# TensorE's order in the loop: value halves among the passes of the inverse, projections ahead of the turning of o, turning of x behind queries times keys

## The reference

```python
x_n = layernorm(x)                             # both parts read this
q, k, v = short_conv_silu(x_n @ Wq/Wk/Wv)      # causal convolution of 4 taps, then silu
beta = sigmoid(x_n @ Wb);  q, k = l2norm(q), l2norm(k)
# delta rule, per head, chunk by chunk, S carried:
A = inverse of (I + strictly lower part of beta k k^T);  u = A (beta v) - A (beta k) S
o = q S + (q k^T, lower part) u;   S = S + k^T u
# multi-scale branch on v: causal convolutions of 3, 15, 31 taps, kernel_mix, channel_mix
# gates: softmax(gelu([x_n, mean |.| of the three branches] @ w1 + b1) @ w2 + b2)
o = gates . (ms, o, v);  o = rms_norm(o);  attention = o @ Wo
# feed-forward: xr, xk = mixes of x_n and the token before
out = sigmoid(xr @ W_r) * (relu(xk @ W_k)^2 @ W_v)
y = x + attention + feed-forward
```

## Time and profile before

| | |
|---|---|
| runs shown | 3519.88 us median, 3506.42 to 3535.21 |
| profiled execution | 3516.6 us, its span 3514.4 us |
| busy share of the span | PE 95%, PE's weight loads 70%, DVE 90%, ACT 78%, POOL 23% |
| chain that ended last | PE 35%, DVE 22%, ACT 21%, issue 10%, DMA 9% |
| mean granted clock of TensorE | 0.98 |

### The profile page before, as it was taken

How to read it: one execution, slowest core, us unless ns; L and a number is a source line. 1 busy time by engine, 2 the same in 40 slices (tenths; PEclk the granted TensorE clock), 3 DMA queues, 4 the chain that set the end, 5 groups by cost and what they waited for, 6 DMA issues and landing times.

```text
span 3514.4 us, 70437 instructions
## 1 busy us (share of the span) xinstructions
PE 3333.0 (95%) x22880; PEld 2459.5 (70%) x22880; DVE 3165.4 (90%) x7841; ACT 2758.5 (78%) x9146; POOL 823.5 (23%) x1501
## 2 busy tenths in 40 slices
PE   7999999999999999999999999999999999999988
PEld 5666777667776677766777767777766777667764
DVE  6998999999988998999989989998999889999994
ACT  5777888778787777877778877788777788777875
POOL 2322221122221222212222112222112222122211
PEclk9999999999999999999999999999999999999999
DMA  6022211122211222112222112221112221122211
GB/s 186 18 40 51 51 35 38 29 51 51 48 29 24 51 51 50 31 32 40 51 51 41 35 26 51 51 50 32 37 33 51 50 47 31 31 44 51 45 30 21
DMA packets 188310, 154.96 MB, mean 44 GB/s; under 512 B 111804, under 2 KB 146108, under 8 KB 187688
## 3 DMA queue, kind: packets, MB, share of 16 engines
q0 software_dynamic: 31744, 79.70, 13.1%
q1 hardware_dynamic: 156200, 70.76, 7.6%
HBM read 51.34 MB, written 52.95 MB: 30 GB/s over the span
## 4 chain that ended last, share of the span: by engine, by line
PE 35%; DVE 22%; ACT 21%; issue 10%; DMA 9%; POOL 3%; SPq 0%; ACTq 0%; DVEq 0%; POOLq 0%
DVE my L1924 16%; PE dense L811 7%; DMA my<-prod 5%; PE dense L734 5%; PE dense L744 5%; PE dense L721 4%; ACT my L1361 3%; PE small L757 2%; DMA rows_out<-Bm 2%; ACT dense L1394 2%; PE cell L703 2%; PE cell L704 2%; POOL Xu L464 1%; DMA Bu<-rows_out 1%; PE cell L696 1%
## 5 line engine op out<-in xcount | busy, mean ns | idle before, releaser
L1924 DVE SCALAR_TENSOR_TENSOR my<-vT,mw,my 128x256 f32<-128x256 f32 x5408 | 2257.1, 482 | 41.1 <-DMA my<-prod 22.3
L422 POOL TENSOR_SCALAR vare<-xsq 128x2 f32<-128x2 f32 x32 | 6.0, 187 | 2037.0 <-ACT xsh L1104 2037.0
L811 PE MATMUL dense<-xsh,w 128*128 128x256 f32 x2016 | 474.5, 381 | 3.8
L811 PEld LDWEIGHTS dense<-xsh,w 128*128 128x128 f32 x2016 | 362.6, 190 | 70.9 <-ACT xr L1426 10.9
L1334 ACT ACTIVATE ka<-dense 128x512 f32<-128x512 f32 x64 | 38.2, 596 | 313.6 <-PE dense L721 313.6
L721 PE MATMUL dense<-xk,wfk 128*128 128x256 f32 x1024 | 249.9, 400 | 11.6 <-DVE xb L1992 10.9
L721 PEld LDWEIGHTS dense<-xk,wfk 128*128 128x128 f32 x1024 | 199.3, 199 | 65.1 <-issue 37.1
L574 PE MATMUL front<-xsh,wq 128*128 128x256 f32 x1024 | 238.2, 386 | 0.6 <-ACT raw L1142 0.6
L734 PE MATMUL dense<-wr,xr 128*128 128x512 f32 x512 | 235.1, 602 | 0.0
L574 PE MATMUL front<-xsh,wv 128*128 128x256 f32 x1024 | 229.9, 382 | 2.7 <-ACT xsh L1119 2.7
L574 PE MATMUL front<-xsh,wk 128*128 128x256 f32 x1024 | 228.2, 379 | 3.8 <-ACT raw L1142 3.8
(11 more groups left out here) (188 smaller groups left out, 6846.2 us busy)
## 6 DMA issues: line engine op xcount, KB each, us to landing
my<-prod POOLq DMA_DIRECT2D x160, 384.0 KB, 4.2
xa<-in_x SPq DMA_DIRECT2D x32, 512.0 KB, 4.4
rows_out<-Bm SPq DMA_DIRECT2D x64, 256.0 KB, 4.2
out<-xb POOLq DMA_DIRECT2D x32, 512.0 KB, 14.8
Yq<-units_out SPq DMA_DIRECT2D x128, 32.0 KB, 2.3
w<-in_w SPq DMA_DIRECT2D x1, 2048.0 KB, 16.2
Bu<-rows_out SPq DMA_DIRECT2D x32, 64.0 KB, 3.1
units_out<-Xu SPq DMA_DIRECT2D x32, 64.0 KB, 2.5
```

The costliest lines, as they stand in the source:

```text
L811: e.matmul(by_batch(o), w1[:, k, hs(2 * pair + c)], xsh[s % 2][:, k, :, 1:1 + P], start=(k == 0), stop=False)
L1924: i = e.scalar_tensor_tensor(o, vT[s % 2][:, c, :, off:off + P], mw[:, col:col + 1], o, ALU.mult, ALU.add)
```

## The change

On TensorE, within the loop only: state(i-2, 0) goes ahead of the second half of value_out(i-2, 1); beta_and_q_norm goes ahead of logits(i-2, 0); turn_tokens(i-1, 2) goes behind kernel_mix(i-1, 0); turn_x(i, 0) goes behind both query_key; key_state(i-1, 1) goes behind the fourth pair of projections; the fifth pair goes ahead of turn_o(i-2, 0); attend(i-2, 0, 0) goes ahead of turn_o(i-2, 1), and the two batches' halves of attend alternate; value_out(i-1, 0, 0) goes ahead of join_Z and its other half between half_W and half_X. In DVE's program adjacent calls of taps with adjoining ranges are written as one call. The programs of ACT, GpSimd and SyncE are not changed.

```diff
@@ -912,8 +912,8 @@
                 gate_out(i - 2, 1, 0)
                 gate_out(i - 2, 1, 1)
                 value_out(i - 2, 1, 0)
+                state(i - 2, 0)
                 value_out(i - 2, 1, 1)
-                state(i - 2, 0)
                 kernel_mix(i - 2, 3)
                 state(i - 2, 1)
                 channel_mix(i - 2, 0, 0)
@@ -933,21 +933,20 @@
                 turn_tokens(i - 1, 1)
                 hidden(i - 2, 3, 0)
                 hidden(i - 2, 3, 1)
+                beta_and_q_norm(i - 1)
                 logits(i - 2, 0)
-                beta_and_q_norm(i - 1)
                 logits(i - 2, 1)
-                turn_tokens(i - 1, 2)
                 turn_logits(i - 2)
                 turn_beta(i - 1)
                 kernel_mix(i - 1, 0)
+                turn_tokens(i - 1, 2)
                 gram(i - 1, 0)
                 gram(i - 1, 1)
-                turn_x(i, 0)
                 query_key(i - 1, 0)
                 query_key(i - 1, 1)
+                turn_x(i, 0)
                 turn_x(i, 1)
                 kernel_mix(i - 1, 1)
-                key_state(i - 1, 1)
                 project(i, 0, 0)
                 project(i, 0, 1)
                 project(i, 1, 0)
@@ -956,13 +955,14 @@
                 project(i, 2, 1)
                 project(i, 3, 0)
                 project(i, 3, 1)
-                turn_o(i - 2, 0)
+                key_state(i - 1, 1)
                 project(i, 4, 0)
                 project(i, 4, 1)
+                turn_o(i - 2, 0)
+                attend(i - 2, 0, 0)
                 turn_o(i - 2, 1)
-                attend(i - 2, 0, 0)
+                attend(i - 2, 1, 0)
                 attend(i - 2, 0, 1)
-                attend(i - 2, 1, 0)
                 attend(i - 2, 1, 1)
                 ffn_key(i - 1, 0, 0)
                 ffn_key(i - 1, 0, 1)
@@ -972,12 +972,12 @@
                 ffn_key(i - 1, 1, 1)
                 join_W(i - 1)
                 turn_tokens(i - 1, 3)
+                value_out(i - 1, 0, 0)
                 join_Z(i - 1)
                 gate_out(i - 1, 0, 0)
                 gate_out(i - 1, 0, 1)
-                value_out(i - 1, 0, 0)
+                half_W(i - 1)
                 value_out(i - 1, 0, 1)
-                half_W(i - 1)
                 half_X(i - 1)
                 key_state(i - 1, 0)
                 solve(i - 1, 1)
@@ -2005,13 +2005,9 @@
             taps(0, 0, 1, 2)
             taps(0, 0, 0, 1)
             taps(0, 0, 2, 3)
-            taps(0, 1, 1, 2)
-            taps(0, 1, 2, 3)
-            taps(0, 1, 4, 5)
-            taps(0, 1, 5, 6)
-            taps(0, 1, 6, 7)
-            taps(0, 0, 3, 4)
-            taps(0, 0, 4, 5)
+            taps(0, 1, 1, 3)
...
```

More of the change, by code:

```diff
@@ L2049, in vector_program @@
             gains(0)
-            taps(0, 1, 23, 24)
-            taps(0, 1, 24, 25)
-            taps(0, 1, 25, 26)
+            taps(0, 1, 23, 26)
             taps(0, 1, 3, 4)
@@ L2055, in vector_program @@
             taps(0, 1, 26, 27)
-            taps(0, 1, 28, 29)
-            taps(0, 1, 29, 30)
+            taps(0, 1, 28, 30)
             taps(0, 2, 5, 6)
@@ L2111, in vector_program @@
             taps(0, 2, 36, 37)
-            taps(0, 2, 49, 50)
-            taps(0, 2, 50, 51)
+            taps(0, 2, 49, 51)
             taps(0, 2, 28, 29)
@@ L2120, in vector_program @@
             taps(0, 3, 1, 2)
-            taps(0, 3, 3, 4)
-            taps(0, 3, 4, 5)
+            taps(0, 3, 3, 5)
             taps(0, 3, 7, 8)
@@ L2135, in vector_program @@
                 turn_Y(i - 2, 1)
-                taps(i - 2, 3, 11, 12)
-                taps(i - 2, 3, 12, 13)
+                taps(i - 2, 3, 11, 13)
                 taps(i - 2, 3, 14, 15)
@@ L2140, in vector_program @@
                 taps(i - 2, 3, 17, 18)
-                taps(i - 2, 3, 15, 16)
-                taps(i - 2, 3, 16, 17)
+                taps(i - 2, 3, 15, 17)
                 taps(i - 2, 3, 20, 21)
@@ L2179, in vector_program @@
                 taps(i - 2, 3, 51, 52)
-                taps(i - 2, 3, 53, 54)
-                taps(i - 2, 3, 54, 55)
+                taps(i - 2, 3, 53, 55)
                 taps(i - 2, 3, 49, 50)
@@ L2187, in vector_program @@
                 taps(i - 2, 3, 55, 56)
-                taps(i - 2, 3, 59, 60)
-                taps(i - 2, 3, 60, 61)
+                taps(i - 2, 3, 59, 61)
                 taps(i - 2, 3, 58, 59)
@@ L2202, in vector_program @@
                 taps(i - 2, 3, 74, 75)
[L2203 to L2207, removed]
+                taps(i - 2, 3, 72, 74)
+                taps(i - 2, 3, 75, 78)
                 short_conv(i - 1, 0, 1)
@@ L2229, in vector_program @@
                 short_conv(i - 1, 5, 3)
[L2230 to L2233, removed]
+                taps(i - 1, 1, 1, 3)
+                taps(i - 1, 1, 4, 6)
                 taps(i - 1, 0, 0, 1)
@@ L2276, in vector_program @@
                 taps(i - 1, 1, 3, 4)
-                taps(i - 1, 1, 28, 29)
-                taps(i - 1, 1, 29, 30)
+                taps(i - 1, 1, 28, 30)
                 make_aT(i - 1, 0)
@@ L2310, in vector_program @@
                 taps(i - 1, 2, 16, 17)
-                taps(i - 1, 2, 38, 39)
-                taps(i - 1, 2, 39, 40)
+                taps(i - 1, 2, 38, 40)
                 taps(i - 1, 2, 19, 20)
@@ L2360, in vector_program @@
             taps(NS - 2, 3, 8, 9)
[L2361 to L2364, removed]
+            taps(NS - 2, 3, 12, 14)
+            taps(NS - 2, 3, 15, 17)
             taps(NS - 2, 3, 11, 12)
@@ L2367, in vector_program @@
             turn_Y(NS - 2, 1)
[L2368 to L2375, removed]
+            taps(NS - 2, 3, 18, 20)
+            taps(NS - 2, 3, 21, 23)
+            taps(NS - 2, 3, 24, 26)
+            taps(NS - 2, 3, 27, 29)
             taps(NS - 2, 3, 14, 15)
@@ L2390, in vector_program @@
             subtract_state(NS - 2, 1)
-            taps(NS - 2, 3, 42, 43)
-            taps(NS - 2, 3, 43, 44)
+            taps(NS - 2, 3, 42, 44)
             taps(NS - 2, 3, 26, 27)
@@ L2420, in vector_program @@
             taps(NS - 2, 3, 59, 60)
-            taps(NS - 2, 3, 61, 62)
-            taps(NS - 2, 3, 62, 63)
+            taps(NS - 2, 3, 61, 63)
             taps(NS - 2, 3, 64, 65)
@@ L2497, in vector_program @@
             taps(NS - 1, 1, 3, 4)
-            taps(NS - 1, 1, 28, 29)
-            taps(NS - 1, 1, 29, 30)
+            taps(NS - 1, 1, 28, 30)
             add_two(NS - 2, 0)
@@ L2553, in vector_program @@
             taps(NS - 1, 2, 28, 29)
-            taps(NS - 1, 2, 44, 45)
-            taps(NS - 1, 2, 45, 46)
+            taps(NS - 1, 2, 44, 46)
             make_aT(NS - 1, 0)
@@ L2565, in vector_program @@
             taps(NS - 1, 3, 3, 4)
-            taps(NS - 1, 3, 5, 6)
-            taps(NS - 1, 3, 6, 7)
+            taps(NS - 1, 3, 5, 7)
             taps(NS - 1, 2, 33, 34)
@@ L2587, in vector_program @@
             taps(NS - 1, 3, 19, 20)
-            taps(NS - 1, 3, 22, 23)
-            taps(NS - 1, 3, 23, 24)
+            taps(NS - 1, 3, 22, 24)
             taps(NS - 1, 3, 18, 19)
@@ L2629, in vector_program @@
             taps(NS - 1, 3, 54, 55)
-            taps(NS - 1, 3, 57, 58)
-            taps(NS - 1, 3, 58, 59)
+            taps(NS - 1, 3, 57, 59)
             taps(NS - 1, 3, 47, 48)
```

66 lines of the change are left out of this document (19 added, 47 removed).

## The result

The changed kernel takes **3532.2 us** (median of 20 runs, 3526.9 to 3540.0) against 3515.9 of the kernel before in the same session: ratio 1.0048, 95% interval 1.0035 to 1.0062. It is slower by about half a per cent; the forecast was 3531, and 11 above the kernel before where 16 were measured. The profiled execution has a span of 3525.0 us against 3514.4.

A forecast was written before the change was run, and what follows sets the result against it. TensorE's in-order work and few waits were taken to make the turn. From the profiled 3516.6 us, +43 for waits, -17 and -8 for the clock and -6 at turn_o gave 3529, stated as 3531 after run spread; range 3500 to 3572.

The forecast's parts named there:

- Two terms: Over the loop: waits add 1.44 us a turn, +43 us in 30 turns; clock and covered waits return 17, 8 and 6.
- its sign: Among the signs that would show the forecast: undisturbed turns of 106.5 to 106.9 us; 105.3 or less would prove it wrong.
- Attends: Projections to ffn_key: new waits of 0.83 and 1.52 us, ffn_key 1.54 later a turn, including 0.44 from the logits moves.
- Logits and turn_x: Logits to kernel_mix(1): moving turn_tokens(2) and turn_x(0) leaves gaps; the two moves share one loss of 0.44 us a turn.
- Value halves: Among the inverse's passes: the 0.68 us wait at L680 goes, 0.9 at value_out comes; -0.1 us a turn.
- The clock: TensorE's 21 falls to 1.2 GHz in the loop: ten at key_state(0) go, -17 us; three turns at inverse_Z, -8.
- The eleven falls at key_state(0): Behind half_W and half_X: a dense half between them removes ten of eleven falls, -17 us, bounds 0 and -19.
- eight at inverse_Z: At inverse_Z: three turns lose their 1.0 us DVE wait and 1.7 us fall, -8 us, bounds 0 and -20.
- both at turn_o: At the turning of o: rare long waits covered up to about 3 us by key_state and fifth pair, -6 us.
- The clock rival: In the loop: all 21 falls and DVE's lateness go, net -4 us, 3512 us; chance 0.11.
- No falls from the new waits: Around the attends: stretches of 0.44 + 0.83 and 0.44 + 1.52 us make no clock falls; bounds 0 and +51 us.

The follow-up runs named there:

- e3: Kernel before with only key_state(1), the projections, turnings of o and attends reordered as in the changed kernel: 3548.3 us, ratio 1.0098.
- e9: Changed kernel with logits, turn_tokens(2) and turn_x ordered as in the kernel before: 3528.8 us, ratio 1.0032.
- e2: Kernel before with only the two value halves moved (ahead of join_Z; between half_W and half_X): 3503.8 us, ratio 0.9968.
- e5: Kernel before with one line moved, the second value half to between half_W and half_X: 3492.1 us, ratio 0.9925.
- e14: e5 with SyncE's copy of x into the output moved from behind read_units to behind subtract_state(0): 3501.2 us, ratio 0.9940.
- e6: e5 with half of the fifth projection pair set ahead of each turning of o: 3496.4 us, ratio 0.9932.
- e10: e3 with the second value half also moved to between half_W and half_X: 3523.6 us, ratio 1.0012.
- e11: e5 with VectorE's subtract_state(0), add_attention(0), turn_Y(0) and mask_W two or three taps earlier: 3501.4 us, ratio 0.9935.
- e13: e11 with ffn_key(0, 1) moved between inverse_W and inverse_Z, and each value half one place later: 3582.0 us, ratio 1.0164.

## Why the prediction was nearly right

The mechanism was right: the waits are where it put them, and their sum outweighs what the clock returns. That the time was met to 1 us is luck. Two terms were too small, and the errors cancelled: +56 instead of +43, and -48 instead of -31. And the start was the 3519.9 of three runs, where twenty gave 3515.9. The undisturbed turn lies outside what the forecast named as its sign, 107.38 for 106.5 to 106.9.

**Attends.** The steps hold to some hundredths: waits of 0.68 and 1.25 for 0.83 and 1.52, ffn_key 10.20 us behind the turning of o for 10.11. But the group costs 1.74 a turn (e3), not 1.10. By places in e3: from project(0) to ffn_key 28.72 (18.52 and 10.20 on either side of the turning of o), where the forecast had 28.43 (18.32 and 10.11) and before has 27.32 in the middle turn (key_state(1) counted in), hence +1.40; and 0.20 of a new wait at project(0), which the forecast never asked for: it walked the new order from project(0) on, and not what key_state(1) had covered for ScalarE. The last 0.14 of the 1.74 is not placed.

**Logits and turn_x.** +0.44 forecast, 0.01 measured on top of the rest (e9 to after). The gap at turn_logits is there (0.72 at L830), but it covers the 0.20 at project(0) and leaves later steps shorter. Two shifts on one path do not add.

**Value halves.** -0.1 forecast, +0.19 measured, the move of state(i-2, 0) included (107.18 in e3, 107.37 in e9). The wait at value_out was 0.69 for 0.9. What failed is the length of the slots: value half and join_Z take 2.54 for 2.35, the gates 3.63 for 3.53, half_W 1.07 for 1.0, the half behind it 1.92 for 1.72. Each of these slots has a change between dense and small products in it and is 0.07 to 0.20 us longer than the forecast read for it among other neighbours; that the change itself costs this is likely, and no run separates it.

**The clock.** The eleven falls at key_state(0) went, as said (ten taken), and e2 and e5 show that the dense half between half_W and half_X did it. Of eight at inverse_Z three were taken as gone, all went; and both at turn_o. The clock rival (all 21) was right on the clock and wrong on the time, as its sum used the same +43. The price was off as well: 1.7 a fall was read from the lower clock alone. A fall at key_state(0) costs 1.25 (e3), but a turn with one at inverse_Z costs about 3.2 (e5: the seven are 0.8 to 6.5 above 105.44), because the stop or the long wait ahead of the fall goes with it. The forecast priced such a wait for three of the eight turns and named the stops ("issue stalls") without a price. They were in the trace of before:

```profile
PE cell L640 <- issue: 6.8, 3, 3.9
```

**No falls from the new waits.** Right: the stretches with 1.32 and 1.09 busy of 2 us kept 1.00 in all 29 turns. The case that the Trainium skill describes ("TensorE: Matmul & The Clock Gate", section "HAM oscillation — how this bites in real kernels") is another one: there the wait for a transfer is longer than the burst of matmuls before it, and the next burst starts at the lower clock. The trace has no such wait at the attends (0.7 and 1.3 us, with 1.7 us of products between), and none at key_state(0) either (0.68 and 0.67 us, behind passes of 1.1), where the clock fell in 11 turns all the same.

**Why the falls at inverse_Z went.** With late attends both things that stand ahead of these falls are gone: in the 29 turns of the changed kernel the longest wait there is 0.76 us and the longest stop 0.43. In the turns in which the kernel before stops (2nd, 9th and 16th), the packet of instructions landed 17.1 to 19.7 us behind the turning of o, past the 16.5 to 16.8 at which inverse_Z starts; in the changed kernel it landed at 13.7 to 15.0, ahead of or with its inverse_Z at 15.0 to 15.2. e3 and e9, with the same attends, kept one stop each (2.07 and 1.03 us), and each had its one fall there.

**What stays open.** Why the packet lands later where the attends are early: that it queues behind the output's DMA was only argued, and e14 moved the wrong transfer. Nor is it known why e3 has 19 falls at key_state(0) where before has 11, with the same two waits in every turn.

## What to carry to other kernels

Undo a change part by part: this one held a gain of 0.3% (value halves) and a loss of 1.0% (attends) whose side effects on the clock partly overlap, and the fastest kernel (e5, -0.75%) is one moved line of it. When an operation is moved out from ahead of another, ask what it covered for the other engines, as well as what it now waits for. When a second engine is 90% busy in a written order, a shorter path on the first is given back at the next operation that takes from that order (e5, e6, e10, e11), so price a saving up to the next hand-over and not beyond.

## What the runs showed of the hardware

- TensorE can stop inside a run of 32 tiny products (64 records of 32x16) that waits for no other engine: 2.22 us after record 46 in e5; in e11 seven such stops hold 21.1 us, the longest 4.5. Each ends 1.2 to 1.6 us behind the landing of a 16 KB packet of instructions (52 stops, 14 traces), and where the clock falls, it falls after the stop.
- A dense half of 1.7 us between two small passes took the falls at that place from 11 to 0 in 29 turns (before to e5), and from 19 to 0 (e3 to e10). It is no guarantee: e13 has dense halves behind both passes and a wait of 1.6 ahead of the first, and 18 falls.
- With the clock in full throughout, the turns of the changed kernel repeat to 0.02 us (107.37 to 107.39 in most); before, they spread from 105.0 to 112.0, and still from 105.0 to 107.2 in the 15 turns without a fall, so the clock is not the whole of it.
